# Feed-forward block of an attention + FFN kernel: the gated values quantised to dense 16-bit integers, transposed by DMA and converted on VectorE

## The reference, cut to what matters

```python
def _act_quant(x):
    scale = 127.0 / jnp.clip(jnp.max(jnp.abs(x), axis=-1, keepdims=True), 0.0001, None)
    return jnp.clip(jnp.round(x * scale), -128, 127) / scale      # value of the straight-through form

def _ternary_quant(w):
    s = jnp.mean(jnp.abs(w))
    return jnp.round(jnp.tanh(w / (s + EPS))) * jnp.arctanh(s)

def _linear_bit(x, w, g):
    return jnp.einsum('bsd,od->bso', _act_quant(_rmsnorm(x, g)), _ternary_quant(w))

x = x + xattn(layernorm(x), ctx_512, Wq, Wkv_expand, Wout)
z = layernorm(x)
h = silu(_linear_bit(z, w1, g1)) * _linear_bit(z, w2, g2)
x = x + _linear_bit(h, w3, g3)
```

## Time and profile before

| | |
|---|---|
| median of 3 runs | 196.1 us (196.01 to 196.95) |
| the profiled execution | 194.6 us |
| its span (first to last instruction in the trace) | 192.9 us |
| lies outside the span | 1.7 us |
| mean granted clock of TensorE | 0.946 of full speed |
| FFN loop: `gated(2)` starts / last `finish` starts | 122.58 us / 190.20 us |

### The profile page before, as it was taken

How to read it: one execution, slowest core, us unless ns; L and a number is a source line. 1 busy time by engine, 2 the same in 40 slices (tenths; PEclk the granted TensorE clock), 3 DMA queues, 4 the chain that set the end, 5 groups by cost and what they waited for, 6 DMA issues and landing times.

```text
span 192.9 us, 3424 instructions
## 1 busy us (share of the span) xinstructions
PE 159.0 (82%) x1122; PEld 107.7 (56%) x1122; DVE 154.0 (80%) x297; ACT 143.2 (74%) x194; POOL 127.7 (66%) x233
## 2 busy tenths in 40 slices
PE   7999599999896985969939989596858998997382
PEld 7585476766584664656725656343524755554261
DVE  0456183999899999999996769798894999999953
ACT  2150968675988869897996798879798999989430
POOL 8281606387464854856617597689987899999810
PEclk9999789999999999999995899979996999999979
DMA  5999970000000000000000000000010000100012
GB/s 166 319 379 378 379 259 0 0 7 0 2 0 0 3 0 0 3 0 2 3 0 0 0 3 0 0 0 28 30 30 28 27 29 31 54 27 31 27 41 70
DMA packets 8241, 11.36 MB, mean 59 GB/s; under 512 B 544, under 2 KB 6944, under 8 KB 8224
## 3 DMA queue, kind: packets, MB, share of 16 engines
q1 hardware_dynamic: 7680, 10.62, 16.0%
q10 hardware_dynamic: 544, 0.52, 1.0%
HBM read 9.04 MB, written 2.10 MB: 58 GB/s over the span
## 4 chain that ended last, share of the span: by engine, by line
DVE 29%; PE 27%; POOL 14%; ACT 13%; issue 12%; DMA 3%; SPq 0%; DVEq 0%; POOLq 0%; ACTq 0%
POOL half_sum L337 6%; DVE hh L1093 5%; DVE c_max L1105 5%; ACT q_x L786 5%; PE bank L476 4%; DVE row_sum L924 4%; PE wide L657 4%; PE bank L493 3%; ACT probsT L746 3%; POOL w_in L426 3%; DMA ctxT<-in_ctxT 3%; ACT probs L766 3%; PE bank L557 3%; PE wide L512 3%; PE bank L579 2%
## 5 line engine op out<-in xcount | busy, mean ns | idle before, releaser
L426 POOL TENSOR_TENSOR w_in<-hh,g3b 128x1024 f32<-128x1024 f32 x15 | 35.8, 2390 | 4.4 <-ACT q_h L851 2.9
L657 PE MATMUL wide<-wT,xqT 128*128 128x512 bf16 x128 | 33.5, 405 | 0.8 <-DVE hh L1093 0.8
L337 POOL TENSOR_TENSOR half_sum<-probs 128x512 f32<-128x512 f32 x16 | 21.1, 1338 | 10.1 <-ACT probs L766 10.0
L476 PE MATMUL bank<-ident,probs 128*128 128x128 f32 x128 | 17.2, 278 | 11.6 <-ACT probsT L746 11.6
L681 PE MATMUL bank<-wT,hT 128*128 128x256 bf16 x128 | 17.6, 283 | 9.0 <-DVE hT L1120 9.0
L851 ACT ACTIVATE q_h<-w_in,round_c,qs_h 128x1024 f32<-128x1024 f32 x16 | 19.8, 1237 | 5.6 <-DVE qs_h L1114 5.6
L476 PEld LDWEIGHTS bank<-ident,probs 128*128 128x128 f32 x128 | 13.8, 141 | 15.8 <-issue 15.6
L681 PEld LDWEIGHTS bank<-wT,hT 128*128 128x128 f16 x128 | 11.7, 100 | 17.0 <-DVE hT L1120 15.1
L657 PEld LDWEIGHTS wide<-wT,xqT 128*128 128x128 bf16 x128 | 12.2, 103 | 15.1 <-issue 3.9
L746 ACT COPY probsT<-bank 128x512 f32<-128x512 f32 x32 | 17.0, 584 | 4.5 <-PE bank L476 4.5
L839 ACT ACTIVATE w_in<-wide,dq_x 128x1024 f32<-128x1024 f32 x16 | 17.7, 1104 | 3.4 <-PE wide L657 3.4
(11 more groups left out here) (139 smaller groups left out, 349.4 us busy)
## 6 DMA issues: line engine op xcount, KB each, us to landing
out<-y SPq DMA_DIRECT2D x16, 128.0 KB, 1.7
w_in<-in_w1T SPq DMA_DIRECT2D x1, 1024.0 KB, 8.6
w_in<-in_w2T SPq DMA_DIRECT2D x1, 1024.0 KB, 12.3
w_in<-in_w3T SPq DMA_DIRECT2D x1, 1024.0 KB, 12.3
xT<-in_xT SPq DMA_DIRECT2D x1, 1024.0 KB, 9.4
x_sb<-in_x SPq DMA_DIRECT2D x1, 1024.0 KB, 11.9
x_sb<-in_x SPq DMA_DIRECT2D x2, 256.0 KB, 5.9
xT<-in_xT SPq DMA_DIRECT2D x1, 512.0 KB, 9.5
```

The lines of the kernel that those rows point to most:

```text
L337: last = g.tensor_tensor(out=half_sum[:, t, :, :], in0=e[:, :, 0, :], in1=e[:, :, 1, :], op=ALU.add)
L426: g.tensor_tensor(out=c_h[:, t, :], in0=hh[:, t, :], in1=g3b[:], op=ALU.mult).then_inc(c_ready, 1)
L476: return nc.tensor.matmul(out, in_, ident[0:n, 0:n], is_transpose=True, start=True, stop=True)
L657: last = nc.tensor.matmul(wide[:, (w * 2 + n) * 512:(w * 2 + n + 1) * 512], xqT[:, T, w * DC + c, :], wT[:, cols:cols + 512], start=(c == ...
```

## The change

The quantised hidden values become dense int16: ACT writes the rounded integer straight to `q_h`, now int16, with no bias. SP transposes the 128 x 1024 tile by one DMA (`dma_start_transpose`) from `q_h` to `hT_int` in SBUF, and DVE converts `hT_int` to bf16 `hT`. The 8 transposing matmuls of each tile, the copy out of PSUM, the column sums and the ninth matmul go. The factor `dq_h` moves from two POOL instructions to one DVE instruction in `hidden_scale`, with a ring of four values; `bound_x` and `bound_h` become two values per token. SP issues the transpose of tile `T` ahead of the store of tile `T-2`.

```diff
 SP
-                for T in range(NT):
+                def hidden_T(T, t):
+                    sp.wait_ge(qh_ready, T + 1)
+                    need(sp, hT_ready, T - 1)
+                    sp.dma_start_transpose(hT_int[:, t, :, :], q_h[:, t, :]).then_inc(hT_landed[t], 16)
+
+                def store(T, t):
                     sp.wait_ge(y_ready, T + 1)
                     sp.dma_start(out_d.rearrange("b s d -> (b s) d")[T * P:(T + 1) * P, :],
-                                 y[:, T % TB, :]).then_inc(stored[T % TB], 16)
+                                 y[:, t, :]).then_inc(stored[t], 16)
+
+                for T in range(NT + 2):
+                    if live_tile(T):
+                        hidden_T(T, T % TB)
+                    if live_tile(T - 2):
+                        store(T - 2, T % TB)
 POOL
-                g.memset(ones_h[:], 1.0)
-                g.memset(offset_h[:], -HALF_ZERO / P).then_inc(half_set, 1)
+                g.memset(w_down[:, 0:1], 127 / CLIP).then_inc(const_set, 1)
...
-                        g.tensor_scalar(m_h[:, before], c_max[:, before], bound_h[:, before], 127.0, ALU.mult,
-                                        ALU.max).then_inc(mh_ready, 1)
...
-                        g.tensor_tensor(out=dq_h[:, before], in0=m_h[:, before], in1=w_down[:],
-                                        op=ALU.mult).then_inc(dqh_ready, 1)
...
+                    g.tensor_tensor(out=bound_h[:, t, :], in0=r_h[:, now].to_broadcast([P, 2]), in1=bound_x[:, b, t, :],
+                                    op=ALU.mult).then_inc(bound_ready, 1)
 PE
-                    for n in range(HC):
-                        last = transposed(hT_banks[t], q_h[:, t, n * P:(n + 1) * P], n)
-                    last.then_inc(hT_done, 1)
...
-                    nc.tensor.matmul(down_banks[t][:, 0:D], offset_h[:], w_col[:],
-                                     start=False, stop=True).then_inc(down_done, 1)
...
-                    if T == 1:
-                        column_sums()
                     if live_tile(T - 2):
                         down(T - 2, t)
-                    if live_tile(T - 1):
-                        hidden_T(T - 1, 1 - t)
 ACT
-                    need(act, hT_done, T - 1)
-                    a.activation(q_h[:, t, :], c_h[:, t, :], ACT.Identity, scale=qs_h[:, t:t + 1],
-                                 bias=round_c[:, 2:3]).then_inc(qh_ready, 1)
+                    need(act, hT_landed[t], 16 * (T // TB))
+                    a.activation(q_h[:, t, :], c_h[:, t, :], ACT.Identity,
+                                 scale=qs_h[:, t:t + 1]).then_inc(qh_ready, 1)
 DVE
+                    v.tensor_scalar(dq_h[:, T % 4:T % 4 + 1], c_max[:, one], bound_h[:, t, 1:2], w_down[:, 2:3],
+                                    ALU.mult, ALU.max).then_inc(dqh_ready, 1)
+
+                def hidden_T_convert(T, t):
+                    need(dve, hT_landed[t], 16 * (T // TB + 1))
                     need(dve, down_done, T - 1)
-                    v.tensor_copy(hT[:, t, :, :].rearrange("p n k -> p (n k)").bitcast(fp32),
-                                  hT_banks[t][:]).then_inc(hT_ready, 1)
+                    v.tensor_copy(hT[:, t, :, :], hT_int[:, t, :, :]).then_inc(hT_ready, 1)
```

More of the change, by code:

```diff
@@ L149, in build_program @@
         ms_h = sb("ms_h", [P, 2])
-        bound_h = sb("bound_h", [P, 2])
-        m_h = sb("m_h", [P, 2])
+        bound_h = sb("bound_h", [P, 2, 2])
         rm_h = sb("rm_h", [P, 2])
         qs_h = sb("qs_h", [P, 2])
[L154 to L159, removed]
+        dq_h = sb("dq_h", [P, 4])
+        q_h = sb("q_h", [P, 2, H], i16)
+        hT_int = sb("hT_int", [P, 2, HC, P], i16)
+        hT = sb("hT", [P, 2, HC, P], bf16)
         y = sb("y", [P, 2, D])
@@ L376, in product_scales @@
                                     None, ALU.mult).then_inc(rootx_ready, n)
-                    g.tensor_scalar(bound_x[:, some, :, :].rearrange("p b t w -> p (b t w)"), flat, 127 / CLIP,
-                                    None, ALU.mult).then_inc(boundx_ready, n)
+                    g.tensor_tensor(out=bound_x[:, some, :, :].rearrange("p b t k -> p (b t) k"),
+                                    in0=dq_x[:, some, :, 1:2].rearrange("p b t w -> p (b t) w").to_broadcast(
+                                        [P, n * TB, 2]),
+                                    in1=w_down[:, 0:2].unsqueeze(1).to_broadcast([P, n * TB, 2]),
+                                    op=ALU.mult).then_inc(boundx_ready, n)
                 pool.wait_ge(sel_in_set, 1)
@@ L428, in scales @@
                 def scales(T, t, b):
[L429 to L432, removed]
[L433 to L451 removed]
+                    now = slice(t, t + 1)
+                    need(pool, sq_ready, T + 1)
+                    g.tensor_scalar(ms_h[:, now], sum_sq[:, now], 1e-8, None, ALU.add).then_inc(ms_ready, 1)
+                    need(pool, ms_ready, T + 1)
+                    g.tensor_tensor(out=r_h[:, now], in0=ms_h[:, now], in1=neg_half[:, 0:1],
+                                    op=ALU.pow).then_inc(r_ready, 1)
+                    need(pool, r_ready, T + 1)
+                    need(pool, boundx_ready, b + 1)
+                    need(pool, dqh_ready, T - 1)
+                    g.tensor_tensor(out=bound_h[:, t, :], in0=r_h[:, now].to_broadcast([P, 2]), in1=bound_x[:, b, t, :],
+                                    op=ALU.mult).then_inc(bound_ready, 1)
                 pool.wait_ge(g3_ld, 16)
@@ L455, in _ @@
                 factor(6)
-                for T in range(NT + 1):
+                for T in range(NT):
                     t, b = T % TB, T // TB
-                    if live_tile(T) and not last_tile(T):
+                    if not last_tile(T):
                         gained(T, t)
@@ L680, in down @@
                     for n in range(HC):
-                        nc.tensor.matmul(down_banks[t][:, 0:D], hT[:, t, n, :], w_cols[:, n, :],
-                                         start=(n == 0), stop=False)
-                    nc.tensor.matmul(down_banks[t][:, 0:D], offset_h[:], w_col[:],
-                                     start=False, stop=True).then_inc(down_done, 1)
-                def column_sums():
-                    pe.wait_ge(half_set, 1)
-                    need(pe, pT_ready, 4 * B)
-                    w_cols = wT[:, 2 * WN:3 * WN].rearrange("p (n o) -> p n o", o=D)
-                    for n in range(HC):
-                        last = nc.tensor.matmul(bank6[:, 0:D], ones_h[:], w_cols[:, n, :],
+                        last = nc.tensor.matmul(down_banks[t][:, 0:D], hT[:, t, n, :], w_cols[:, n, :],
                                                 start=(n == 0), stop=(n == HC - 1))
-                    last.then_inc(col_done, 1)
+                    last.then_inc(down_done, 1)
                 pe.wait_ge(tern_ready, 3)
@@ L805, in _ @@
                 abs_sums(1)
-                act.wait_ge(half_set, 1)
+                act.wait_ge(const_set, 1)
                 def iteration(j):
```

48 lines of the change are left out of this document (16 added, 32 removed).

## The result

The changed kernel takes 202.89 us (median of 4 runs, 202.39 to 204.28); the kernel before took 196.52 beside it (196.01 to 199.21). The ratio is 1.034, with an interval of 1.027 to 1.042: slower by 6.8 us. The profiled execution took 202.39 us, with a span of 200.5.

A forecast was written before the change was run, and what follows sets the result against it. DVE was taken to bound the FFN loop at 3.69 us per tile. Terms 8.6 + 1.4 + 2.9 + 1.5 - 1.0 = +13.4 us on the profiled 194.6 made 208.0, plus 1.5 for the median: 209.5 us, range 200 to 236.

The forecast's parts named there:

- the forecast's own case: Whole kernel: both waits occur, with a landing between 1.7 and 5 us; 203 to 218 us, chance 0.58.
- Rival 2: DVE's conversion and POOL's c_h do not clash over ports, the landing alone decides; 197 to 203 us if short, chance 0.03.
- First wait: FFN steady tiles: DVE's conversion stands until POOL's c_h ends; step 4.35 us, 0.66 more on 13 tiles, +8.6 us.
- Tile 4: ACT reaches q_h late there, so the landing is uncovered: 5.3 us from q_h to conversion instead of 2.36, +2.9 us.
- The conversion by itself: DVE's int16 to bf16 pass replacing the PSUM copy: 0.43 us, of which 0.35 counts in the order.
- Second wait: Steady tiles wait for the transposing DMA's landing: 0.2 to 0.25 us per pair of tiles, six pairs, +1.4 us.
- L: Time from the transposing DMA's issue to its landing: 4.0 us, with 1.7 to 12.9 as ends.
- rival 1: The DMA transpose is far slower than a plain DMA: 243 us at an 8 us landing; above 218 us, chance 0.28.
- Tail: Last tile: 5.3 us from q_h to conversion instead of 3.44, less 0.4 for shorter conversion and missing matmul; +1.5 us.
- Head: Column sums before the first qs_h go; -1.0 us counted of 1.65.
- The third: Rival claiming a faster kernel: no port clash and a landing under 2.2 us; 193 us, chance 0.06.
- The fourth: Rival on PE's clock: more waiting makes PE's lower clock level the rule, some +7 us more; 216 us, chance 0.03.

The follow-up runs named there:

- e1: Changed kernel, but the conversion reads a constant tile and waits for no DMA, while the transposes still run; 198.43 us, ratio 1.006.
- e3: Changed kernel with constants converted without waiting for the DMA, over 9 blocks into an output with gaps; 194.59 us, ratio 0.984.
- e6: Changed kernel with the conversion over 9 blocks, one of them filler, into an output with gaps (repeat run); 201.54 us, ratio 1.031.
- e7: Changed kernel with POOL multiplying only 512 of the 1024 columns of c_h; 198.27 us, ratio 1.020.
- e9: From e4, every second tile's transposing DMA cut into four of 256 columns; 210.65 us in one run.
- e4: Changed kernel without conversion: q_h holds fp16 bit patterns, transposed by DMA straight into PE's tile; column sums and ninth matmul return; 192.50 us, ratio 0.975.

## Why the prediction was right, and where its sizes were off

The measured 202.89 us lies near the low end of the range (200 to 236) and 0.1 us below what the forecast's own case was to give alone (203 to 218); the change is half of the +13.4 us forecast. Rival 2, no clash, gives 202 us for the landing of 3.1 that was measured, so the time alone would speak for that rival. That the range holds the time is in part luck. What was right is the mechanism, and it is the held conversions and the runs that show it.

**First wait.** Right in place and cause: e1, e3, e6 and e7 show it by four different edits. Predicted were steps of 4.35 us; measured 4.24. The own time left after `c_h`'s end was put at 0.35 and is 0.20 (175.90 to `y` at 176.10), and `c_h` ends 3.64 us after `hh` began instead of 3.61. The term of +8.6 came out as +6.6: 12 steps (+2.32 and +4.27 in the table) of 0.55 us on the mean, not 13 of 0.66. Tile 4's step, which I counted here too, has its own term, and the two steps that the landing ends are among the 12. Of the +2.32 in the first four steps, among which attention work lies, +1.63 is the one step from `hh(3)` to `hh(4)`, 7.08 us against 5.45, with the conversion held for 2.17. That is the same wait: e1, without a landing, has 7.08 there too, and e3, with neither wait, 5.30.

**The conversion by itself.** Estimated 0.43, measured 0.42 to 0.43 where it is free. The held ones are 0.6 us longer, one of them 1.7; I had looked for 0.8.

**Second wait.** L was put at 4.0 us and is 3.1, the quiet 256 KB load's time. I had said that up to 3.8 is covered by the first wait; e1 confirms that at 3.1 it is in the steady tiles. Only the two steps after tile 4 (158.61 and 163.04) are ended by it, for some 0.2 us together, which is counted in the +6.6; the term of +1.4 has nothing beyond that. For L = 3.1 the prediction names a sum of about +9; its own terms give 8.6 + 0 + 2.1 + 0.6 - 1.0 = +10.3, so the landing explains only part of the miss. "Advanced Engine Details and Errata", X-Bar Transpose, in the Trainium skill, by which a transposing DMA is as fast as a plain one, agrees with that load, 3.1 us for both, but not with the stores: in e9 a quarter, 64 KB, lands in 2.4 us and a plain store of 128 KB in 2.0. The eight blocks in a row of rival 1, worked out from 1309 ns for one block (the Trainium skill, "VectorE: DVE Perf Modes", The three transpose paths), do not occur: in e9 two blocks land in 2.4 us, in the other kernels eight in 3.1 (medians).

**Tile 4.** From the start of `q_h` to the conversion it is 150.05 - 145.76 = 4.29 us, against 5.3 predicted and 2.36 before: +1.93, of which only +0.45 reaches the next `hh`. The rest was an error of the reckoning: before, PE's up products stood behind the transposes that waited for this `q_h`, and `hh(7)` came 1.77 us after the copy (146.48 to 148.25); now they do not, and `hh(7)` comes 0.73 after the conversion. Of the 1.04 us between, 0.69 was DVE's wait for those up products, the rest lies in the shorter conversion and `y`. The transposes on PE, which I called worth nothing as such, were worth 0.69 us at this one place:

```profile
148.25 1.22 DVE L1093 TENSOR_TENSOR hh<-w_in,wide 128x1024 f32<-128x1024 f32 x1 [0.69 <-PE wide L657]
```

PE had idled 2.45 us before these transposes and ran at a granted clock of 0.65 from 146.2 to 149.2 (2.92 us for the up products against 1.90). At the higher level the half of them that `hh(7)` needs would by an estimate have ended near 147.2 (146.23 + 0.95), before DVE was done with `y` at 147.56, so the 0.69 us is by this estimate the price of PE's clock as much as of the order. `q_h` also comes sooner after `hh(6)`, by 0.44.

**Tail.** Conversion 195.80 - 191.52 = 4.28 us after `q_h`, against 3.44 before: +0.84. With L = 3.1 in place of 4.0 my 5.3 would have been 4.4. The 0.4 us that the shorter conversion and the missing matmul should give back do not show: from there to the end it takes 4.70 us, and 4.65 before. The rows of PE for the last `down`, after and then before, show where they go:

```profile
196.28 1.55 PE L664 MATMUL bank<-wT,hT 128*128 128x256 bf16 x8 [0.55 <-DVE hT L1091]
...
189.00 1.05 PE L681 MATMUL bank<-wT,hT 128*128 128x256 bf16 x8 [0.79 <-DVE hT L1120]
189.88 0.27 PE L683 MATMUL bank<-w_col,offset_h 128*128 128x256 f16 x1
```

PE starts 0.48 us after the conversion where it started 0.75 after the copy, which gives 0.27 back. But before the last tiles PE now idles more and runs at the lower of its two levels (granted clock 0.50 in the window from 189 to 193, 0.66 during the last `down` against 1.00 before), so that eight matmuls take 1.55 us where nine took 1.15.

**Head.** -1.0 predicted, -1.51 measured: nearly all of the 1.65 us came back.

Together: 6.6 + 0 + 0.45 + 0.8 - 1.5 = +6.3 where I had +13.4. The mechanism that decides was named. Of the 7.1 us between, 4.6 lie in the three terms of the landing (1.4, 2.45 and 0.7; at tile 4 in part for the reason above), 2.0 in the first wait and 0.5 at the head.

**The rivals.** The second is confirmed as a mechanism by e7: without the clash the step should be (4.9 + 3.1) / 2 = 4.0, and is 3.93. The third's condition was put as no clash and a landing under 2.2 us; e3, with both gone, is faster than before, though its conversion alone is 0.3 us longer and its step, 3.93, longer than the 3.57 of that rival. The fourth did not come: the granted clock is 1.00 in the steady tile, and the lower level costs some 0.4 us in the tail alone.

## What to carry to other kernels

Before work goes to an idle path, look at what stands on the neighbouring engine at that very time: a cast in SBUF that takes 0.43 us alone takes 1.04 behind a 2.35 us product on GpSimd, and a form that is slower alone (0.74) can be the faster one (e3 against e1: 194.6 against 198.4 us). Where two waits cover each other, removing either shows little; take both away once, with constants if need be, to see what the change could bring. And if the data can be given the bit pattern that the consumer reads, a DMA transpose needs no conversion behind it: here that is 192.5 us against 202.9.

## What the hardware did that I had not expected

* A transposing DMA between SBUF tiles costs mostly a fixed part: 2.4 us for 128 x 256 elements of 2 bytes, 3.1 for 128 x 1024; 1.24 us of each is SP's own instruction, and in e9 the store behind four of them goes out 5.08 us after the first (158.03 to 163.11).
* A store of 128 KB lands in 2.0 us (median) among the transposes, 1.7 without them.
* ACT's quantising pass is 0.1 us shorter without a bias: `q_h` takes 1.14 us on the mean in the changed kernel, and 1.24 both in the kernel before (fp32 out, bias) and in e4 (int16 out, bias).
